# Dual attention over four images: three places for exponentials, two landing buffers, x1 by halves of queries

## What is computed

```python
# block 0, per image, x [256, 1024]
h = group_norm(x, 32 groups) * gn_w + gn_b
q, k, v = wq @ h + bq, wk @ h + bk, wv @ h + bv
w = softmax((q.T @ k) / sqrt(256), axis=-1)      # [1024, 1024]
x1 = x + wo @ (v @ w.T) + bo
# block 1
att = x1 @ x1.T                                  # [256, 256]
feat_e = softmax(max(att) - att) @ x1
fb, fc, fd = wb @ x1 + bb, wc @ x1 + bc, wd @ x1 + bd     # fb, fc: 32 rows
s = softmax(fb.T @ fc, axis=-1)                  # [1024, 1024]
out = (beta * feat_e + x1) + (alpha * (fd @ s.T) + x1)
```

## Time and profile before

| | us |
|---|---|
| median of the runs | 443.41 (443.25 to 443.66) |
| profiled execution, its own time | 444.55 |
| its span, first to last instruction | 442.6 |
| TensorE busy in the span | 418.5 |
| VectorE, ScalarE, GpSimd busy | 305.8, 239.2, 54.2 |

### The profile page before, as it was taken

The page is one execution under the profiler, slowest core; times in us unless marked ns, Lnnn a source line. Parts: engine busy times, 40 slices in busy tenths (PEclk is TensorE's granted clock), DMA queues, the critical chain, the costliest instruction groups (busy, mean ns, idle before and its releaser), DMA issues.

```text
span 442.6 us, 5658 instructions
## 1 busy us (share of the span) xinstructions
PE 418.5 (95%) x2090; PEld 283.8 (64%) x2090; DVE 305.8 (69%) x468; ACT 239.2 (54%) x312; POOL 54.2 (12%) x51
## 2 busy tenths in 40 slices
PE   2999999999999999999999999999999998898975
PEld 2888856576687555767858555777658545556442
DVE  3468787587889696765979785566879566688411
ACT  1548562556674755574675652575577545566300
POOL 1300061030000500120100510500000002000000
PEclk9979999999999999999999999999999999999999
DMA  8445448532063787533795469132397754057731
GB/s 232 149 137 83 83 90 199 93 73 49 0 130 66 188 185 140 96 73 30 159 175 95 90 142 151 32 65 47 68 230 130 123 125 87 0 95 134 153 96 47
DMA packets 140395, 48.02 MB, mean 108 GB/s; under 512 B 135824, under 2 KB 137296, under 8 KB 140368
## 3 DMA queue, kind: packets, MB, share of 16 engines
q1 hardware_dynamic: 136400, 36.52, 45.0%
q0 software_dynamic: 2144, 7.34, 5.1%
q10 hardware_dynamic: 1824, 3.80, 2.7%
HBM read 9.90 MB, written 4.19 MB: 32 GB/s over the span
## 4 chain that ended last, share of the span: by engine, by line
PE 73%; DVE 10%; DMA 5%; ACT 5%; issue 4%; POOL 2%; SPq 0%; POOLq 0%; ACTq 0%; DVEq 0%
PE score_ps L805 11%; PE score_ps L807 11%; PE score_ps L806 11%; PE sum_ps L805 10%; PE sum_ps L806 10%; PE sum_ps L807 10%; DVE pieces L682 3%; PE score_ps L960 2%; PE score_ps L930 2%; DVE negmax L666 2%; DMA x<-in_x_dram 2%; DMA x<-in_L_conv_wo_dram 2%; PE score_ps L815 1%; POOL xn_l L348 1%; DMA land<-pieces 1%
## 5 line engine op out<-in xcount | busy, mean ns | idle before, releaser
L429 ACT ACTIVATE exps<-score_ps,negmax 128x1024 f32<-128x1024 f32 x64 | 71.1, 1111 | 81.9 <-DVE negmax L666 66.1
L682 DVE SCALAR_TENSOR_TENSOR pieces<-exps,recip,pieces 128x1024 f16<-128x1024 f32 x64 | 88.6, 1388 | 23.6 <-ACT pieces L439 23.5
L666 DVE TENSOR_REDUCE negmax<-score_ps 128x1 f32<-128x1024 f32 x64 | 77.2, 1217 | 18.1 <-PE score_ps L807 13.0
L439 ACT ACTIVATE pieces<-exps,recip 128x1024 f16<-128x1024 f32 x64 | 72.7, 1144 | 26.8 <-DMA land<-pieces 21.3
L805 PE MATMUL score_ps<-xn_h,g_h 128*128 128x512 f32 x128 | 53.1, 415 | 0.2 <-DVE g_l L533 0.2
L807 PE MATMUL score_ps<-xn_h,g_l 128*128 128x512 f32 x128 | 50.6, 395 | 0.0
L806 PE MATMUL score_ps<-xn_l,g_h 128*128 128x512 f32 x128 | 50.6, 395 | 0.0
L805 PE MATMUL sum_ps<-land,fd_h 128*128 128x512 f16 x128 | 48.8, 381 | 1.5 <-DMA land<-pieces 1.5
L805 PE MATMUL sum_ps<-land,v_h 128*128 128x512 f16 x128 | 48.7, 380 | 0.3 <-DVE x L771 0.3
L807 PE MATMUL sum_ps<-land,fd_l 128*128 128x512 f16 x128 | 48.5, 379 | 0.0
L806 PE MATMUL sum_ps<-land,fd_h 128*128 128x512 f16 x128 | 48.5, 379 | 0.0
(11 more groups left out here) (169 smaller groups left out, 754.5 us busy)
## 6 DMA issues: line engine op xcount, KB each, us to landing
out_dram<-x POOLq DMA_DIRECT2D x16, 256.0 KB, 3.0
x<-in_x_dram ACTq DMA_DIRECT2D x6, 512.0 KB, 4.4
x_in<-in_x_dram POOLq DMA_DIRECT2D x6, 512.0 KB, 5.5
x_in<-in_x_dram SPq DMA_DIRECT2D x2, 512.0 KB, 4.5
x<-in_x_dram SPq DMA_DIRECT2D x2, 512.0 KB, 4.5
land<-pieces SPq DMA_TRANSPOSE x64, 4.4
x<-in_L_conv_wk_dram ACTq DMA_DIRECT2D x1, 256.0 KB, 4.0
x<-in_L_conv_wo_dram SPq DMA_DIRECT2D x1, 256.0 KB, 7.4
```

Source lines behind the costliest of these rows:

```text
L429: act.activation(exps[:, n % 2, :], score_ps[s][:, :], ACT.Exp, bias=negmax[:, n % RING:n % RING + 1], scale=1.0, accum_out=rowsum[:, n % ...
L439: act.activation(pieces[:, n % 2, 0, :], exps[:, n % 2, :], ACT.Copy, scale=recip[:, n % RING:n % RING + 1]).then_inc(high_piece, 1)
L666: dve.tensor_reduce(negmax[:, n % RING:n % RING + 1], score_ps[s][:, :], AX.X, ALU.max, negate=True)\
L682: dve.scalar_tensor_tensor(pieces[:, n % 2, 1, :], exps[:, n % 2, :], recip[:, n % RING:n % RING + 1], pieces[:, n % 2, 0, :], ALU.mult, A ...
```

## The change

- `exps` and `pieces` get 3 places (`AHEAD`), `land` gets 2 buffers (`HALVES`): a transpose for sum k waits for the end of sum k-2.
- x1 is split by halves of the queries: `x1h.b.c` and `x1l.b.c` treat both channel blocks of 512 queries, and wait for the sums of that half alone. `FBC` becomes two steps of 6 matmuls, each with its own score buffer, `hFBC` two steps of three copies of 512 columns and `lFBC` two of two. `XT.b.u` waits for half u alone, `FD.b.u` for the split of half u. Both halves of FBC must be done before an S2 tile.
- All four orders are written anew. The last image on PE (`-` before, `+` after), and with it the parts of ACT's and DVE's orders that the prediction speaks of:

```diff
 PE_ORDER
-    S2.2.7 O0.3.1x8 O2.2.1x1 XT.3.0 XT.3.1 FBC.3 ATT.3 O2.2.1x1 S2.3.0 S2.3.1 AT.3
-    O2.2.1x1 S2.3.2 S2.3.3 O2.2.1x3 S2.3.4 O2.2.1x2 MX.3 FD.3.0 ET.3 S2.3.5 O2.2.1x1 S2.3.6 FD.3.1 O2.2.1x1
-    O2.3.0x6 S2.3.7 O2.3.0x4 O2.3.1x10
+    S2.2.7 O0.3.1x6 XT.3.0 O0.3.1x2 O2.2.1x1 XT.3.1 FBC.3.0 FBC.3.1 ATT.3 S2.3.0 S2.3.1 O2.2.1x2 S2.3.2
+    O2.2.1x2 S2.3.3 O2.2.1x1 MX.3 AT.3 S2.3.4 FD.3.0 O2.2.1x4 S2.3.5 ET.3 FD.3.1 O2.3.0x2 S2.3.6 S2.3.7 O2.3.0x8
+    O2.3.1x10
...
+    O0.0.0x6 G.1.0 O0.0.0x2 S0.1.0 S0.1.1 O0.0.1x1 MEAN.2 O0.0.1x1 S0.1.2 O0.0.1x5 S0.1.3 O0.0.1x1 FBC.0.0 V.1.0
+    G.1.1 MX.0 V.1.1 FBC.0.1 XT.0.0 O0.1.0x2 VAR.2 S2.0.0 S2.0.1 O0.1.0x1 S2.0.2 O0.1.0x1 XT.0.1 FD.0.0 S2.0.3
...
+    O2.0.1x1 AT.1 S2.1.1 O2.0.1x1 V.2.1 O0.2.0x1 S2.1.2 O0.2.0x1 S0.2.4 O0.2.0x2 S2.1.3 S0.2.5 O0.2.0x2 S0.2.6
+    O0.2.0x1 FD.1.0 O0.2.0x1 ET.1 S0.2.7 XT.2.0 FD.1.1 O2.1.0x2 S2.1.4 O2.1.0x3 S2.1.5 O2.1.0x1 S2.1.6 G.3.0
+    S2.1.7 O2.1.0x4 S0.3.0 O0.2.1x8 S0.3.1 O2.1.1x4 S0.3.2 S0.3.3 O2.1.1x3 MX.2 O2.1.1x2 FBC.2.0 O2.1.1x1
 ACT_ORDER
+    exp0.2.4 exp2.1.3 a2.1.2 a0.2.4 xb.2.1 exp0.2.5 a2.1.3 exp0.2.6 a0.2.5 hFD.1.0 hET.1 xnh.3.0 hXT.2.0
...
+    a2.1.6 exp0.3.0 a2.1.7 a0.3.0 exp0.3.1 x1h.2.1 a0.3.1 exp0.3.2 a0.3.2 exp0.3.3 a0.3.3 hFBC.2.0 hFBC.2.1
...
+    x1h.3.0 exp0.3.7 exp2.2.4 a0.3.7 a2.2.4 exp2.2.5 a2.2.5 exp2.2.6 exp2.2.7 a2.2.6 a2.2.7 hXT.3.0 x1h.3.1
+    hXT.3.1 hFBC.3.0 base.3.0 hFBC.3.1 base.3.1 cA.3 exp2.3.0 exp2.3.1 a2.3.0 exp2.3.2 a2.3.1 a2.3.2 exp2.3.3
+    exp2.3.4 expE.3 hFD.3.0 a2.3.3 a2.3.4 hET.3 exp2.3.5 hFD.3.1 a2.3.5 exp2.3.6 exp2.3.7 a2.3.6 a2.3.7
 DVE_ORDER
+    max2.2.5 r2.2.5 max2.2.6 b2.2.5 fo.2.0.0 fo.2.0.1 max2.2.7 r2.2.6 r2.2.7 b2.2.6 b2.2.7 lXT.3.0 fx.3.1.0
+    fx.3.1.1 mx.3 x1l.3.1 lXT.3.1 lFBC.3.0 lFBC.3.1 sA.3 max2.3.0 max2.3.1 r2.3.0 max2.3.2 r2.3.1 b2.3.0 r2.3.2
+    max2.3.3 b2.3.1 sF.3 aA.3 max2.3.4 minE.3 b2.3.2 r2.3.3 nE.3 lFD.3.0 b2.3.3 r2.3.4 fo.2.1.0 fo.2.1.1
```

The code's part (`AHEAD = 3` and `HALVES = 2` stand at the top):

```diff
-        exps = sb("exps", [P, 2, N])
-        pieces = sb("pieces", [P, 2, 2, N], f16)
+        exps = sb("exps", [P, AHEAD, N])
+        pieces = sb("pieces", [P, AHEAD, 2, N], f16)
...
         x1_high, x1_read, base_made = sem("x1_high"), sem("x1_read"), sem("base_made")
-        x1_split = several("x1_split", CH)
+        x1_split = several("x1_split", CHUNKS)
...
                     land[:, k % HALVES, :, :, cols(j)].rearrange("p a t q -> p (a t) q"),
-                    pieces[:, n % 2, :, :].rearrange("p a n -> p (a n)")).then_inc(landed[k % HALVES][j], 16)
+                    pieces[:, n % AHEAD, :, :].rearrange("p a n -> p (a n)")).then_inc(landed[k % HALVES][j], 16)
...
                 elif name == "x1l":
-                    b, m = n
-                    pool.wait_ge(x1_high, b * CH + m + 1)
+                    b, c = n
+                    half = cols(c, QC)
                     x1_h_b, x1_l_b = x1_parts(b)
-                    pool.tensor_tensor(x1_l_b[:, m, :], x1s[b % 2][:, m, :], x1_h_b[:, m, :].bitcast(f32), ALU.subtract)\
-                        .then_inc(x1_split[m], 1)
+                    pool.wait_ge(x1_high, b * CHUNKS + c + 1)
+                    pool.tensor_tensor(x1_l_b[:, :, half], x1s[b % 2][:, :, half], x1_h_b[:, :, half].bitcast(f32),
+                                       ALU.subtract).then_inc(x1_split[c], 1)
...
                 s, _, staged = SCORE[use]
-                if n >= 2:
-                    act.wait_ge(both_pieces, n - 1)
+                if n >= AHEAD:
+                    act.wait_ge(both_pieces, n - AHEAD + 1)
                 act.wait_ge(score_staged[s], staged + 1)
-                act.activation(exps[:, n % 2, :], score_ps[s][:, :], ACT.Exp, bias=negmax[:, n % RING:n % RING + 1],
+                act.activation(exps[:, n % AHEAD, :], score_ps[s][:, :], ACT.Exp, bias=negmax[:, n % RING:n % RING + 1],
...
                 n = TILE[use]
-                if n >= 2:
-                    k, j = turn_of(TILES[n - 2])
+                if n >= AHEAD:
+                    k, j = turn_of(TILES[n - AHEAD])
...
                 act.wait_ge(recip_made, n + 1)
-                act.activation(pieces[:, n % 2, 0, :], exps[:, n % 2, :], ACT.Copy,
+                act.activation(pieces[:, n % AHEAD, 0, :], exps[:, n % AHEAD, :], ACT.Copy,
...
                     s, ps = full(step[1:])
-                    high(fb_parts[0:2 * C8, :], ps[0:2 * C8, :], bbc_bias[0:2 * C8, :])
-                    high(fc_parts[0:C8, :], ps[2 * C8:3 * C8, :], bbc_bias[2 * C8:3 * C8, :])
-                    high(fc_parts[2 * C8:3 * C8, :], ps[2 * C8:3 * C8, :], bbc_bias[2 * C8:3 * C8, :])\
+                    half = cols(n[1], QC)
+                    high(fb_parts[0:2 * C8, half], ps[0:2 * C8, 0:QC], bbc_bias[0:2 * C8, :])
+                    high(fc_parts[0:C8, half], ps[2 * C8:3 * C8, 0:QC], bbc_bias[2 * C8:3 * C8, :])
+                    high(fc_parts[2 * C8:3 * C8, half], ps[2 * C8:3 * C8, 0:QC], bbc_bias[2 * C8:3 * C8, :])\
...
                 elif name == "x1h":
-                    b, m = n
-                    act.wait_ge(sum_done[m], sum_of(0, b, 1) + 1)
+                    b, c = n
+                    half = cols(c, QC)
+                    for m in range(CH):
+                        act.wait_ge(sum_done[m], sum_of(0, b, c) + 1)
...
                     elif b:
-                        act.wait_ge(x1_read, b)
-                    high(x1_parts(b)[0][:, m, :], x1s[b % 2][:, m, :]).then_inc(x1_high, 1)
+                        act.wait_ge(x1_read, (b - 1) * CHUNKS + c + 1)
+                    high(x1_parts(b)[0][:, :, half], x1s[b % 2][:, :, half]).then_inc(x1_high, 1)
...
                         full(f"XT.{b}.{u}")
-                    act.wait_ge(x1_split[m], b + 1)
+                    for c in range(CHUNKS):
+                        act.wait_ge(x1_split[c], b + 1)
...
                 dve.wait_ge(high_piece, n + 1)
-                dve.scalar_tensor_tensor(pieces[:, n % 2, 1, :], exps[:, n % 2, :], recip[:, n % RING:n % RING + 1],
-                                         pieces[:, n % 2, 0, :], ALU.mult, ALU.subtract).then_inc(both_pieces, 1)
+                dve.scalar_tensor_tensor(pieces[:, n % AHEAD, 1, :], exps[:, n % AHEAD, :], recip[:, n % RING:n % RING + 1],
+                                         pieces[:, n % AHEAD, 0, :], ALU.mult, ALU.subtract).then_inc(both_pieces, 1)
...
                     s, ps = staged(step[1:])
-                    low(fb_parts[2 * C8:3 * C8, :], ps[0:C8, :], fb_parts[0:C8, :], bbc_bias[0:C8, :])
-                    low(fc_parts[C8:2 * C8, :], ps[2 * C8:3 * C8, :], fc_parts[2 * C8:3 * C8, :],
+                    half = cols(n[1], QC)
+                    low(fb_parts[2 * C8:3 * C8, half], ps[0:C8, 0:QC], fb_parts[0:C8, half], bbc_bias[0:C8, :])
+                    low(fc_parts[C8:2 * C8, half], ps[2 * C8:3 * C8, 0:QC], fc_parts[2 * C8:3 * C8, half],
...
                 elif name == "x1l":
-                    b, m = n
+                    b, c = n
+                    half = cols(c, QC)
                     x1_h_b, x1_l_b = x1_parts(b)
-                    dve.wait_ge(x1_high, b * CH + m + 1)
-                    low(x1_l_b[:, m, :], x1s[b % 2][:, m, :], x1_h_b[:, m, :]).then_inc(x1_split[m], 1)
+                    dve.wait_ge(x1_high, b * CHUNKS + c + 1)
+                    low(x1_l_b[:, :, half], x1s[b % 2][:, :, half], x1_h_b[:, :, half]).then_inc(x1_split[c], 1)
...
-            def x1_ready(b):
-                for m in range(CH):
-                    pe.wait_ge(x1_split[m], b + 1)
+            def x1_ready(b, c):
+                pe.wait_ge(x1_split[c], b + 1)
...
             def scores2(use, b, j):
-                done(f"FBC.{b}")
+                for c in range(CHUNKS):
+                    done(f"FBC.{b}.{c}")
...
                 for m in range(CH):
-                    pe.wait_ge(sum_done[m], sum_of(0, b, 1) + 1)
+                    pe.wait_ge(sum_done[m], sum_of(0, b, u) + 1)
...
-            def project_fbc(use, b):
-                x1_ready(b)
+            def project_fbc(use, b, c):
+                x1_ready(b, c)
                 s, ps = enter(use)
-                for n in range(2):
-                    for k in range(CH):
-                        last = product(ps[0:3 * C8, cols(n, QC)], both(bbc_w, every, k, every),
-                                       both(x1_parts(b), every, k, cols(n, QC)), k == 0, k == CH - 1)
+                for k in range(CH):
+                    last = product(ps[0:3 * C8, 0:QC], both(bbc_w, every, k, every),
+                                   both(x1_parts(b), every, k, cols(c, QC)), k == 0, k == CH - 1)
...
                                        both(x1_parts(b), every, i, cols(c, QC)), i == 0, False)
-                    if c == CHUNKS - 1 and m == CH - 1:
+                    if m == CH - 1:
...
                 elif name == "FD":
-                    x1_ready(n[0])
+                    x1_ready(*n)
```

94 lines of the change are left out of this document (42 added, 52 removed).

## The result

The changed kernel takes 438.36 us (median of four runs, 436.21 to 439.22) where the kernel before takes 443.54 (median of four; the 443.41 above is that of its first three): a ratio of 0.9873 (0.9834 to 0.9912). Forecast were 438.5 us, in 436.5 to 442.0. The number came out right; several of its terms did not, and they happened to cancel. The profiled execution of after lies at the lower end of its runs, 436.21 us with a span of 434.3, that of before above its median, with 442.6. The two traces are 8.3 us apart and the medians 5.2, so the first question is what of the 8.3 belongs to the change.

What follows compares the result with a forecast made beforehand. Only PE's 24.1 us of standing still could be won, nearly all in the last 75 us. Tail 4.7 + batch 0 0.4 + boundary 0.1 - reload 0.3 = 4.9 us off the median 443.41 gives 438.5 us, range 436.5 to 442.0.

Steps and rivals of the forecast that it cites:

- fx.3.1 to S2.3.0: Last batch's tail: first S2 score starts 11.5 us after the first fx.3.1 addition, 3.2 us sooner; PE stands some 0.4.
- E: Moment when the first of the last two fx.3.1 additions begins, 367.98 us in the kernel before; tail times count from it.
- Halves of queries: Tail: FBC.3.0, x1h.3.0, XT.3.0 and low parts need only the first 512 queries' sums, done 10 us earlier.
- S2.3.4, 0.8 us: Tail: S2.3.4 finds its score buffer not free, as exp2.3.3 stands behind a2.3.1 and a2.3.2 on ACT; 0.8 us stop.
- The wait for fo.3.0.0 stays, 1.15 us: Tail, late in the last batch: PE's stop for the fo.3.0.0 addition remains, 1.15 us.
- The middle: Between start and tail: in batch 0, stops of 0.3 and 0.6 us become about 0.5 at S2.0.1; gain 0.4 us.
- The boundary: At 358 us: of a 0.3 us stop 0.1 goes, since max2.2.6 no longer stands before fo.2.0.0.
- Three places, "no gain by itself": Exponentials and pieces: ACT's waits for a landing go, but PE waited for none in the middle; nothing gained.
- Landing buffers at nothing: Three landing buffers to two: cost nothing; tightest S2.1.3, with 9.9 us for 6.3, 3.5 us late at the worst row.
- Reloading x1, 0.3 us: Ahead of XT.2.0: work queued on ACT behind the x1 reload delays fx.2.0.0; 0.3 us lost, nothing with a quick load.
- More instructions: FBC's extra copies: 0.25 us each, 0.8 us a batch on ACT and 0.4 on DVE, off the path except in the tail.
- The port: Rival: more POOL subtractions meet DVE low pieces, 2.15 us each; one before a tight place gives 440.6 us; chance 0.13.

Runs made afterwards that it cites:

- the run with the late half: Changed kernel with XT.3.0, x1h.3.0, hXT.3.0 and lXT.3.0 moved back behind the last image's first-block sum; 438.97 us, ratio 0.9898 to before.
- One move in the old kernel: Kernel before with score tile S2.3.7 behind two steps of O2.3.0 on PE instead of six; 440.59 us, ratio 0.9926 to before.
- the run with the third piece: Kernel before with the changed kernel's order from ATT.3 on and a third place for pieces; 445.56 us, ratio 1.0043 to before.
- that with three landings: Changed kernel with pieces back at two places and land at three buffers, abs_w laid over xt; 458.91 us, ratio 1.0342 to before.

## Why the prediction was right, and where it was not

- **What bounds the kernel**: right. PE's stops behind 358 us were the gain, 5.5 of 6.2 us in the traces.
- **fx.3.1 to S2.3.0, E + 11.5**: measured E + 11.8. `mx` was the first limit and ACT's queue the second, as forecast. `mx` and its diagonal end at E + 4.1 for E + 4.5, so FBC.3.1 starts 0.6 us sooner than forecast and its stop is 0.53 for 0.9. "Three small copies take 1.9 us with their overlap" was too little: they take 0.68 + 1.38 = 2.07 each time, without overlap, and with the low parts that makes S2.3.0 0.3 us later. With PE 0.6 sooner there and the scores 0.3 later, the stop at S2.3.0 is 1.26 for 0.4.
- **Halves of queries**: the credit was given to the right piece, the smaller FBC, but the first point, that "before E there are one XT and one x1 split more", is worth nothing, as the run with the late half shows. Of the 3.2 us by which S2.3.0 was to come sooner behind E, 1.1 is E moving; from O0.3.1 it comes 1.8 us sooner. The old code with the new tail's order has none of this (24.7 us), and the late half all of it (22.7), so it goes with FBC by halves; that it is the copies starting after six matmuls instead of twelve is read from the traces.
- **S2.3.4, 0.8 us**: 0.83. S2.3.5, ET.3 and the rest found what they needed, as forecast.
- **"The wait for fo.3.0.0 stays, 1.15 us"**: wrong. It is 0.36, since the last low piece no longer stands before it. One move in the old kernel shows 0.84 us for it. The landing's 1.55 is covered, as forecast. With these the tail gave 5.5 us for 4.7, and the stops behind E add up to 3.5 us for 3.9.
- **The middle**: from 40 to 350 us PE waits 1.3 us in after and 1.7 in before, the forecast 0.4. The starts of the steps give 1.1; the other 0.7 lies in gaps that are not booked as waits, and I have not taken them apart. In the two further profiles of these orders the gain up to O0.3.1, boundary included, is 0.0 and -0.2 for 0.7 here, mostly by the reload. **The boundary** is wrong in sign: 0.1 us was to be won because max2.2.6 no longer stood before `fo.2.0.0`, but in the new order both it and b2.2.5 do, and the stop grew from 0.30 to 0.73. I read the old order for what the step is behind, and not the new one.
- **Three places, "no gain by itself"**: true of the old orders (no gain with a third piece). Yet the step stopped there. The new orders with two pieces, and three landing buffers, lose 21 us, and even the new tail alone loses 3.2. It cost the forecast nothing, because the change brings both, but as a reading it missed what the orders rest on.
- **Landing buffers at nothing**: no PE stop on `land` in after. The tight places that I named, S2.1.3 and O2.1.1, held: S2.1.3's tile landed at 241.5 and was used at 244.1. SP held transposes back for a landing buffer nine times, 37.2 us in all, and no PE stop came of it. The place that is tight is S0.1.3, which I did not check because two buffers do not touch it; the order of DVE does. It cost nothing in the three profiles of these orders, and 1.7 us in two kernels near them.
- **Reloading x1, 0.3 us**: 0 to 2.5 in seven profiles, mean 0.8. Right mechanism, more than twice the size; the forecast took one time to land, and it was 6.8 to 10.9 us.
- **More instructions**: ACT's busy time rose 3.5 us, of which 4 x 0.8 = 3.2 was forecast. The copies of 512 columns take 0.68 each, so the rows' 0.25 us an instruction is right. The 0.14 us, an estimate from the Trainium skill (VectorE: DVE Perf Modes, The TRN2 errata), is too little here.
- **The port**: not a rival that came true, though the meetings doubled. The low pieces of after, beside a middle value of 1.28 us before:

```profile
L690 DVE SCALAR_TENSOR_TENSOR pieces<-exps,recip,pieces 128x1024 f16<-128x1024 f32 x64 | 91.4, 1440 | 19.3 <-ACT pieces L443 19.0
```

  64 x (1.440 - 1.283) = 10.0 us of DVE standing at the port, nearly all in six pieces of 2.4 to 3.45 us, where before had three. No PE stop follows any of them. The Trainium skill (SBUF — State Buffer, SBUF: two separate sides) has it that the later of the two is blocked for the whole of the other's instruction; the trace agrees.
- **The sum.** 4.7 + 0.4 + 0.1 - 0.3 = 4.9 was measured as 5.2 us, and as 6.5 for the same kernel again. By the traces the terms are 5.5 in the tail, 1.1 in the middle and -0.4 at the boundary, and from that the reload takes 0 in the profile of after, 0.6 and 0.8 in the other two of these orders. The tail's gain was taken 0.8 too low and the middle's 0.7, the boundary's 0.5 too high, and the reload 0.3 to 0.5 too cheap. These errors cancel in part, and that is why the number came out so near: that much of it is luck. That the gain lies in the tail's stops is not.

## What to carry to other kernels

When an order and its buffers change together, ask of each buffer what the **new** order does with the old count, not what the old order did with it: the wait that a place removes may exist only there. Before a stop is booked as "stays", look at what stands before its releaser in that engine's queue, since two stops in a row are often one late tile; a single move of that tile is the cheapest test, and here it gave 2.4 of the tail's 5.5 us. Give every moved tile a landing distance that also holds when a transfer takes half as long again.

## What the runs showed of the hardware

- **Long stops can cost twice.** PE after the two stops of 2.42 and 4.40 us, in the kernel before with the new tail's order:

```profile
384.00:388.00 4.00, 4.00 (x13) 0.58 0.00 0
...
397.00:405.00 8.00, 6.51 (x29) 0.57 0.49 91
```

  The granted clock is 0.58 and 0.57 there, so most of these stretches is at 1.2 GHz; in before (stops up to 1.55 us) it is 1.00 from 29 us to the end of the matmuls. Standing and slow clock together made its tail 5.6 us longer than before's; PE stood 2.4 us more, and the rest goes with the clock. The same fall was there in the run with the third piece, after stops of 2.42 and 3.00 us, which I had given a chance to escape it, and four times in that with three landings, at stops of 2.1, 2.0, 3.5 and 4.4 us. But the stop of 2.2 us at O0.1.0, in two other kernels, was followed by none, so the length of a stop alone doesn't decide it.
- **Instruction packets can delay a transpose's landing**: 4.26 us alone, 4.86 in the middle and up to 6.3 with an instruction packet between issue and landing (16 KB, 0.9 us in the case shown). This is a comparison across traces, not of a run that moved a packet. What places the packet stays open.
- **The clock at the start** makes runs of one kernel differ by up to 2 us; the time at the lower level was 3.4 or 6.8 us and nothing between. In the thirteen profiles the old orders' start had the short stretch in two of five and the new ones' in five of eight. A pair of single profiles of this kernel can't be compared closer than that unless its start is taken out.
